# Order of ScalarE's copies, gates and roundings, and of VectorE's last row sums and remainders, between the recurrence and the experts

## The reference, cut to what matters

```python
xk = x_prev + (x - x_prev) * tmk              # xv, xr alike
k, v, r = xk @ Wk.T + bk, xv @ Wv.T + bv, xr @ Wr.T + br
# for each channel, over time, with a running maximum for safety:
#   out = (e1 * aa + e2 * v) / (e1 * bb + e2);  aa, bb decay by exp(-exp(time_decay))
x = layernorm(x + (sigmoid(r) * wkv(k, v)) @ Wo.T + bo)
logits = x @ wg                               # 8 experts
expert = argmax(logits); gate = softmax(logits)[expert]
x = layernorm(x + gate * (W[expert] @ x + b[expert]))
```

## Time and profile before

| | |
|---|---|
| median of 3 runs | 624.85 us (624.83 to 629.8) |
| profiled execution, its own time | 624.3 us |
| its span, first to last instruction | 622.6 us |
| mean granted TensorE clock | 0.972 of full speed |
| TensorE busy | 565.3 us, 91% |
| VectorE busy | 542.3 us, 87% |
| ScalarE busy | 428.2 us, 69% |
| GpSimd busy | 273.7 us, 44% |

### The profile page before, as it was taken

How to read it: one execution, slowest core, us unless ns; L and a number is a source line. 1 busy time by engine, 2 the same in 40 slices (tenths; PEclk the granted TensorE clock), 3 DMA queues, 4 the chain that set the end, 5 groups by cost and what they waited for, 6 DMA issues and landing times. The chain is left out here.

```text
span 622.6 us, 9016 instructions
## 1 busy us (share of the span) xinstructions
PE 565.3 (91%) x2452; PEld 419.3 (67%) x2453; DVE 542.3 (87%) x862; ACT 428.2 (69%) x806; POOL 273.7 (44%) x217
## 2 busy tenths in 40 slices
PE   1777879999999999999999999998998999999991
PEld 0555656677668768767866876775456878788880
DVE  6988898998999999899999989878998898777770
ACT  4637465586677758768776775946777676788872
POOL 2164445452553445446155444511032465766631
PEclk9797989999999999999999999999988999999996
DMA  8373071047109306602810930667555686878740
GB/s 300 113 183 82 0 181 23 2 169 135 35 13 241 86 0 203 117 17 92 206 39 0 241 98 2 199 139 270 168 181 158 178 235 211 247 243 221 239 157 0
DMA packets 40980, 84.41 MB, mean 136 GB/s; under 512 B 8751, under 2 KB 8751, under 8 KB 40818
## 3 DMA queue, kind: packets, MB, share of 16 engines
q1 hardware_dynamic: 30482, 56.67, 27.9%
q0 software_dynamic: 10464, 27.33, 20.1%
HBM read 66.95 MB, written 35.65 MB: 165 GB/s over the span
## 5 line engine op out<-in xcount | busy, mean ns | idle before, releaser
L1110 POOL TENSOR_TENSOR mixed<-unsplit,mixed 128x1024 fp32r<-128x1024 f32 x44 | 106.5, 2442 | 149.1 <-ACT mixed L762 149.1
L516 PE MATMUL kb<-mixed,w_kvr 128*128 128x512 f32 x384 | 98.6, 408 | 21.2 <-DVE w_kvr L1450 13.8
L516 PE MATMUL vb<-mixed,w_kvr 128*128 128x512 f32 x384 | 101.7, 416 | 11.3 <-DVE evn L1292 11.2
L692 PE MATMUL y_ps<-w_e_hi,xgT 128*128 x312 | 109.0, 410 | 0.6 <-issue 0.4
L516 PE MATMUL rb<-mixed,w_kvr 128*128 128x512 f32 x384 | 98.8, 406 | 5.3 <-DVE ee L1306 5.1
L529 PE MATMUL y_ps<-w_o,rw 128*128 128x512 f32 x224 | 100.8, 594 | 0.0
L516 PEld LDWEIGHTS kb<-mixed,w_kvr 128*128 128x128 f32 x384 | 73.8, 196 | 39.8 <-issue 13.5
L516 PEld LDWEIGHTS vb<-mixed,w_kvr 128*128 128x128 f32 x384 | 73.6, 196 | 32.5 <-DVE evn L1292 14.7
L516 PEld LDWEIGHTS rb<-mixed,w_kvr 128*128 128x128 f32 x384 | 71.9, 189 | 26.8 <-DVE ee L1306 6.3
L1126 POOL TENSOR_TENSOR ee<-ee,state 128x512 f32<-128x512 f32 x32 | 34.9, 1091 | 94.1 <-DVE state L1276 93.3
L1243 DVE SCALAR_TENSOR_TENSOR unsplit<-diff,vec,xb 128x512 f32<-128x512 f32 x96 | 65.8, 746 | 6.4 <-PE kb L516 6.1
(11 more groups left out here) (230 smaller groups left out, 1037.7 us busy)
## 6 DMA issues: line engine op xcount, KB each, us to landing
bias<-b_experts SPq DMA_DIRECT2D x39, 256.0 KB, 4.4
x_biased<-bo POOLq DMA_DIRECT2D x8, 1024.0 KB, 17.3
w_e_raw<-w_experts SPq DMA_DIRECT2D x8, 1024.0 KB, 8.1
rows<-x_biased SPq DMA_DIRECT2D x28, 256.0 KB, 3.1
x_rows<-rows SPq DMA_DIRECT2D x28, 256.0 KB, 6.4
xb<-xT SPq DMA_DIRECT2D x4, 1026.0 KB, 5.3
xb<-xT SPq DMA_DIRECT2D x3, 1024.0 KB, 5.1
w_raw<-w_square SPq DMA_DIRECT2D x2, 1024.0 KB, 10.6
```

Source lines behind the costliest of these rows:

```text
L516: mm = pe.matmul(bank, w_kvr[m][:, a, h, o:o + P], mixed[m][:, bb, h, :], start=(k == 0), stop=(k == 3 * CH - 1))
L692: mm = pe.matmul(y_ps[:, n % 2, :], xgT[n % 3][:, a, c, :], w[:, bass.ds(p, 1), c, :].rearrange("p u o -> p (u o)"), start=(c == 0 and (a, ...
L1110: pool.tensor_tensor(mixed[m][:, LO, 2 * hp:2 * hp + 2, :], unsplit[m][:, LO, 2 * hp:2 * hp + 2, :], mixed[m][:, HI, 2 * hp:2 * hp + 2, :] ...
```

## The change

Only the order of instructions on ScalarE and VectorE changes; each engine does the same work. On ScalarE: `move_turned(earlier, 3)` goes ahead of `entry_weight(last, 2)`; `expert_hi(0)` with its wait on `k_filled` goes ahead of `reciprocal_guess(last, 0)`; `gate_r(last, 2)` goes ahead of `decay` and `weight` of chunk 3; `move_turned(before, 0)` goes ahead of `deviation_before(1)`, `move_turned(before, 1)` ahead of `expert_hi(5)`, `move_turned(before, 3)` behind `norm_last(1)`. On VectorE: `add_last(1)` goes directly behind `add_last(0)`, and `expert_lo(5)` ahead of the first gathered tile's split.

```diff
--- before.py
+++ after.py
@@ -1015,22 +1015,22 @@
             move_turned(earlier, 2)
 
             enter_q(3, *here)
+            move_turned(earlier, 3)
             entry_weight(last, 2)
-            move_turned(earlier, 3)
             decay(last, 2)
             weight(last, 2)
             enter_ab(last, 2, *here)
             gate_r(last, 1)
             gates_of(1)
-            reciprocal_guess(last, 0)
-
             act.wait_ge(k_filled, CHUNKS)
             expert_hi(0)
+            reciprocal_guess(last, 0)
+
             entry_weight(last, 3)
+            gate_r(last, 2)
             decay(last, 3)
             weight(last, 3)
             enter_ab(last, 3, *here)
-            gate_r(last, 2)
             expert_hi(1)
 
             gate_r(last, 3)
@@ -1041,20 +1041,20 @@
             act.wait_ge(r_filled, CHUNKS)
             expert_hi(2)
             expert_hi(3)
+            move_turned(before, 0)
             deviation_before(1)
             norm(before, 1)
-            move_turned(before, 0)
             expert_hi(4)
+            move_turned(before, 1)
             expert_hi(5)
-            move_turned(before, 1)
             act.wait_ge(y_filled, last * TPB)
             expert_hi(6)
             deviation_last(0)
             norm_last(0)
             move_turned(before, 2)
-            move_turned(before, 3)
             deviation_last(1)
             norm_last(1)
+            move_turned(before, 3)
 
             def move_gathered(k, n):
                 act.wait_ge(turned, k + 1)
@@ -1647,10 +1647,11 @@
             dve.tensor_scalar(ids_full[:, :, 0], lists_ps[:, 0:FULL], -1.0, None, ALU.add).then_inc(ids_ready, 1)
             tile_experts(FULL, taken[:, 1:], iota_row, after_full, expert_full, slot_full)
             add_last(0)
+            add_last(1)
             expert_lo(2)
             expert_lo(3)
-            add_last(1)
             expert_lo(4)
+            expert_lo(5)
 
             def choose_late():
                 largest(EARLY, LATE, late_ps, lg2)
@@ -1749,7 +1750,6 @@
             add_last(2)
             add_last(3)
             split_gathered(1, 1)
-            expert_lo(5)
             expert_lo(6)
             expert_lo(7)
             add_bias(0, 0, 0)
```

## The result

The changed kernel takes 621.02 us in the median of 10 executions (620.28 to 622.8), against 624.84 us for the kernel before (10 executions, 624.05 to 629.8). The ratio is 0.992, with a 95% interval of 0.9901 to 0.9939. The medians differ by 3.8 us and the lowest times by 3.8 us. The profiled execution took 622.48 us, 620.8 of them its span.

A forecast was written before the change was run, and what follows sets the result against it. TensorE waits only 0.4 us in the last 136 us, so time won at the first expert tile reaches the end. Gains 1.52 + 1.59 + 0 + 0.58 = 3.69 us, from 624.85 to 621.15 us; range 619.0 to 623.1.

The forecast's parts named there:

- Edit 1: Fourth turned copy ahead of the third chunk's entry weight: TensorE's wait before the fourth logits goes, gain 1.52 us.
- Edits 2 and 3: ScalarE: 2, expert 0's rounding ahead of the guess; 3, third gate ahead of decay and weight; VectorE's 1.59 us wait goes.
- Edit 4: ScalarE's copies of the block before the last and roundings 4 to 6 reordered: TensorE's 1.07 us wait goes, gain 0.
- Edit 5: VectorE's second row sum forward, remainder 5 ahead of the first gathered split: 2.78 us wait becomes 2.2 work, gain 0.58.
- a kinder clock: Case for the whole kernel's time: 619.0 to 619.9 us, chance 0.18.
- a worse one: Case of a worse clock for the whole kernel's time: 622.2 to 623.1 us, chance 0.10.
- the main range: Whole kernel's time if the forecast holds with small errors of its terms: 620.3 to 622.1 us, chance 0.56.
- Rival 2: GpSimd's gathers starve behind four VectorE subtractions in a row: 624.8 us, or 626.1 if the second is caught; chance 0.05.
- signs of being wrong: First split still waits for ScalarE, gathers of 5 us appear, or TensorE waits anew between 486 us and the end.
- Rival 3: Expert 0's rounding runs into the reciprocal guess on ScalarE: up to 1.9 us return, 623.05 us; chance 0.06.

The follow-up runs named there:

- e1: Kernel before with only the fourth turned copy moved ahead of the third chunk's entry weight; ratio 0.9998 (0.9976-1.002).
- e9: Kernel before with only the fourth turned copy, expert 0's rounding and the third gate moved as in the change; ratio 0.9962 (0.9929-0.9995).
- e5: Kernel after with the rounding of expert 0 put back behind the reciprocal guess; ratio 0.990 (0.9851-0.9948).
- e6: Kernel after with the third gate put back behind decay, weight and `enter_ab`; ratio 0.9883 (0.9834-0.9932).
- e10: Kernel after with ScalarE's three copies of the block before the last back in their old places; ratio 0.9955 (0.9916-0.9995).
- e3: Kernel before with only ScalarE's copies of the block before the last, VectorE's second row sum and remainder 5 moved; ratio 0.9983 (0.9964-1.0003).
- e12: Kernel after run once more, unchanged, on the chip of three other runs; ratio to the kernel before 0.9931 (0.990-0.9962).
- e4: Kernel after with expert 5's remainder put back behind the second gathered split; median 619.4 us, ratio 0.9902 (0.9868-0.9936).
- e7: Kernel after with 12 unread matmuls of 512 columns added on TensorE between the second and third turning; ratio 0.993 (0.9889-0.9971).
- e11: Kernel after with expert 5's remainder put back and four unread matmuls ahead of each of the last two logits of the block before the last; ratio 0.9898.
- e2: Kernel before with only expert 0's rounding moved ahead of the guess and the third gate ahead of decay and weight; ratio 0.9981 (0.9958-1.0005).
- e8: Kernel after with the remainders of experts 4 and 5 both put back behind the second gathered split; ratio 0.9893 (0.9863-0.9922).

## Why the prediction was right, by its steps

**The size.** 3.69 us were forecast, 621.15 us (624.85 less 3.69 is 621.16); the medians moved by 3.8, to 621.02. The pair of profiles gives 3.3, from two errors against each other: 0.4 more at the split, 0.8 less in the first expert tile. The mechanism was right, wait by wait; that the median came within 0.2 us of the forecast is partly luck, since the executions of after alone range over 2.5 us and the clock took back 0.8 us that the sum did not have.

**Edit 1** was put at 1.52 us and measured 1.77 (e1). The counted wait is not the whole stall: behind a wait the logits took 1.06 us instead of 0.95, and without one they start 0.16 us before the projection's modelled end (410.62 + 3.01 = 413.63 against 413.47).

**Edits 2 and 3** were put at 1.59 together, and measured 1.68 (e1 to e9: 21.12 to 19.44). The step that failed is their split into parts: "What the edit brings is that the 1.90 us no longer stand between the guess and the third gate" reads as if edit 3 needed edit 2. It doesn't; each alone leaves no wait (e5, e6).

**Edit 4** was put at 0, "Nothing lost, nothing won". In the changed kernel that failed: without it the first split is 0.64 us later (e10). Edit 4 without edit 5 was not run. The prediction's own count for edit 5 ran ScalarE in the new order, row tile 1 ahead of the last copy, and so used edit 4 without booking it.

**Edit 5** was put at 0.58; with edit 4 it brings 0.64 (e3, and e9 against e12), and without it nothing (e10). That VectorE would be late next was right, and remainder 5 ahead of the split costs 2.23 us there (e4), which the prediction had as a price of 2.2. The 0.64 us of the two edits are shown at the split only. At the third tile nothing is left of them, +73.08 without (e9) against +73.30 and +73.11 with them (after, e12), and +76.56 against +76.74 (before, e3), since the first tile was slower; the medians of e9 and e12 differ by 0.2 us.

**The clock.** The prediction's chances hold a kinder clock, 619.0 to 619.9, and a worse one, 622.2 to 623.1. No run shows the terms that lead to these two ranges. What the runs showed in their place is the length of the first expert tile: 4.43 us before, 2.86 at a granted clock of 1.00 (e7), so 1.57 less, and 5.26 at 0.50 (after), so 0.83 more. The unkind half came: one spell of 10.2 us, and those 0.83 us; the median still fell into the main range. Ahead of the tile TensorE's single idle stretches are shorter after (0.82, 0.94 and 1.53 us, against 2.19 before), but the work between them is thin from 462.8 on (1.14 to 1.60 us busy of each 2 us from 462 to 472). That the thin stretch causes the long spell is the theory of e7 and e11, and no run shows it. For it speak the mean clocks of e11 (0.976 to 0.979 in seven of nine executions, against 0.969 to 0.972 in e12), and that the spells of 10.2 us came only in profiles without an earlier one (after, e3, e6, e12). Against it: e4, with the order of e11 and no fill, has no spell there either (its one of 3.4 us came earlier), and e5 has a spell of 6.8 us from +42.8, where after, e6 and e12 have none with the same work on TensorE up to there. **Rival 2** did not come: gathers took 1.9 to 2.0 us beside the subtractions, each was issued in time, and the rest is as long as before, 136.9 us against 136.8. One of the prediction's own signs of being wrong did come: TensorE waits anew behind 486 us, three times for a gather (0.36, 0.27 and 0.35 us at 508.61, 536.14 and 539.94), where before it had one wait of 0.40. **Rival 3** did not come in the kernel after, but its mechanism showed in e2, 0.90 us.

## What to carry to other kernels

Walk a reorder through all engines from one wait to the next and ask at each who is late next; the sum so made held to 0.4 us at the first split over five edits, but which edit earns a term shows only when each is undone in the changed kernel: here two could each do the other's work, and one was worth nothing without its neighbour. Work that is due anyway still costs its whole length when it stands ahead of the first thing that the bounding engine needs; moved behind that, it can still be in the way of the next (e4, e8). Where an effect is below the spread of the times, compare places in the profile from a common point ahead of the edits, and read the granted clock before believing either.

## What the hardware showed that was not expected

- The granted clock moves this kernel as much as the edits do. Between +42 and +71 us the profiles show half-speed spells of 3.4 us (twice in before, e1, e9 and e10, once in e4), 6.8 us (e7, e8, twice in e2, and in e5 beside one of 3.4), 10.2 us (after, e3, e6, e12) and none (e11), and the length of the same first expert tile ran from 2.86 to 5.27 us.
- Within a batch, executions of one kernel differ with the mean clock: before, 623.3 to 625.9 us at 0.972 to 0.976 and 625.7 to 629.5 at 0.970 and less (batch of e1 to e4).
- Chips differ in the stretch of the expert tiles: 136.3 to 136.9 us from the third tile to the end in six profiles (before, after, e1 to e4), 142.5 to 145.5 in the eight others. Why was not tried. The profiles do show that TensorE then no longer runs there nearly without waits, on which the prediction had built: the waits listed behind 484 us sum to 5.0 us in e12, against 1.0 in after. How much of a gain at the first tile reaches the end on those chips was not measured.
